# An exponential split between ScalarE and VectorE: six-pass VectorE blocks, six a unit instead of five, and a shorter accumulator read-out and quantisation

## The reference

```python
xn = _layernorm(x)
q, k, v = (split_heads(xn @ w.T + b) for w, b in ...)      # 16 heads of 16; q is divided by sqrt(16)
attn = softmax(einsum('bhqd,bhkd->bhqk', q, k))            # 4096 x 4096 for each head
ctx = einsum('bhqk,bhkd->bhqd', attn, v)
x_fp8 = clip(xn * scale, -448, 448).astype(float8_e4m3fn)  # the same for the weight
out = x + (ctx @ out_w.T + out_b) + ((x_fp8 @ w_fp8.T) * scales + bias)
```

## Time and profile before

| | us |
|---|---|
| median of 3 runs | 1886.2 (1885.57 to 1886.49) |
| span of the profiled execution, first to last instruction | 1883.1 |
| outside the span, against the median | 3.1 |
| ScalarE's exponentials, first start to last end | 108.9 to 1840.2 |
| busy: PE, DVE, ACT | 1648.8, 1552.4, 1764.1 |

### The profile page before, as it was taken

How to read it: one execution, slowest core, us unless ns; L and a number is a source line. 1 busy time by engine, 2 the same in 40 slices (tenths; PEclk the granted TensorE clock), 3 DMA queues, 4 the chain that set the end, 5 groups by cost and what they waited for, 6 DMA issues and landing times.

```text
span 1883.1 us, 74604 instructions
## 1 busy us (share of the span) xinstructions
PE 1648.8 (88%) x33418; PEld 558.0 (30%) x33418; DVE 1552.4 (82%) x1908; ACT 1764.1 (94%) x1944; POOL 41.1 (2%) x57
## 2 busy tenths in 40 slices
PE   7988888888888888888888888888888888888888
PEld 4632222222222222222222222222222222222226
DVE  8687878878787888878787987878888887878786
ACT  2389999999999999999999999999999999999990
POOL 0000000000000000000000000000000000000003
PEclk9999999999999999999999999999999999999999
DMA  7420100000000100000010000001000000001003
GB/s 202 154 90 10 32 10 22 13 18 24 18 24 10 24 13 16 24 18 24 10 31 8 17 20 18 24 10 31 10 22 12 18 24 18 24 10 26 13 14 107
DMA packets 94966, 57.20 MB, mean 30 GB/s; under 512 B 55280, under 2 KB 87280, under 8 KB 94640
## 3 DMA queue, kind: packets, MB, share of 16 engines
q1 hardware_dynamic: 94160, 52.18, 10.3%
q10 hardware_dynamic: 480, 0.20, 0.0%
HBM read 30.54 MB, written 17.30 MB: 25 GB/s over the span
## 4 chain that ended last, share of the span: by engine, by line
ACT 48%; issue 37%; PE 11%; DVE 1%; POOL 1%; ACTq 1%; DMA 0%; SPq 0%; POOLq 0%; DVEq 0%
ACT probs L679 48%; PE banks L1308 3%; PE banks L1164 3%; PE banks L1267 3%; PE banks L1175 1%; ACTq L678 1%; DVE o_junk L963 1%; DVE o_sb L962 1%; POOL o_sb L600 0%; PE banks L1148 0%; POOL o_junk L600 0%; DMA qk_bias<-in_L_attn_k_b_dram 0%; DVE bits L983 0%; DVE w_max L764 0%; DVE xn_all L833 0%
## 5 line engine op out<-in xcount | busy, mean ns | idle before, releaser
L679 ACT ACTIVATE probs<-banks 128x1024 f32<-128x1024 f32 x1888 | 1731.0, 1193 | 0.3 <-PE banks L1267 0.2
L1308 PE MATMUL banks<-probs,v_st 64*32 64x512 f32 x15104 | 1004.5, 590 | 2.2
L1267 PE MATMUL banks<-q_st,k_st 50*32 50x512 f16 x16384 | 793.3, 381 | 211.9 <-ACT probs L679 208.9
L1267 PEld LDWEIGHTS banks<-q_st,k_st 50*32 50x32 f16 x16384 | 233.5, 89 | 1145.3 <-ACT probs L679 1088.8
L996 DVE SCALAR_TENSOR_TENSOR horner<-horner,bits 128x1024 f32<-128x1024 f32 x320 | 393.1, 1228 | 11.0
L1308 PEld LDWEIGHTS banks<-probs,v_st 64*32 64x32 f32 x15104 | 272.3, 106 | 66.4 <-DVE o_junk L963 11.4
L983 DVE TENSOR_SCALAR bits<-banks 128x1024 int32<-128x1024 f32 x160 | 195.9, 1225 | 76.9 <-PE banks L1267 76.8
L996 DVE SCALAR_TENSOR_TENSOR horner<-bits 128x1024 f32<-128x1024 f32 x160 | 196.1, 1226 | 5.5
L1001 DVE SCALAR_TENSOR_TENSOR d_probs<-horner,powers 128x1024 f32<-128x1024 f32 x160 | 196.0, 1225 | 5.5
L962 DVE COPY o_sb<-banks 128x512 f32<-128x512 f32 x32 | 22.1, 692 | 130.9 <-PE banks L1308 98.0
L992 DVE TENSOR_SCALAR bits<-bits 128x1024 int32<-128x1024 int32 x160 | 111.1, 694 | 5.5
(11 more groups left out here) (103 smaller groups left out, 435.6 us busy)
## 6 DMA issues: line engine op xcount, KB each, us to landing
k_st<-k_parts SPq DMA_DIRECT2D x102, 64.0 KB, 2.2
q_st<-q_parts SPq DMA_DIRECT2D x198, 32.0 KB, 1.9
k_st<-k_parts SPq DMA_DIRECT2D x102, 60.0 KB, 2.2
q_st<-neg_row SPq DMA_DIRECT2D x264, 1.0 KB, 1.7
xnT_copy<-probs SPq DMA_DIRECT2D x8, 512.0 KB, 3.1
q_parts<-x8T SPq DMA_DIRECT2D x16, 256.0 KB, 2.9
k_parts<-x8T SPq DMA_DIRECT2D x16, 256.0 KB, 2.4
w_f<-xnT_copy SPq DMA_DIRECT2D x16, 256.0 KB, 2.9
```

The lines of the kernel that those rows point to most:

```text
L679: act.activation(probs[:, at:at + WIDE * CHUNK].rearrange("p (t c) -> p t c", t=WIDE), banks[:, bank:bank + WIDE, :], ACT.Exp, bias=EXP_SHIFT,
L1267: last = pe.matmul(banks[cols, bank + g, :], k_st[rows, keys], blocks[rows, j], start=True, stop=True, tile_position=(g * GROUP, t * VCOLS))
L1308: last = pe.matmul(banks[VCOLS * qb:VCOLS * (qb + 1), 6 + half, cols], v_st[keys, kt, :], src[keys, g * CHUNK:(g + 1) * CHUNK][:, cols], s ...
```

## The change

Four things, all in VectorE's program and in the constants:

1. `d_block` has six passes instead of seven: out of the bank into integers (as before), one mask (fraction bits), then four two-operand passes, three on f32 for a cubic in the fraction and a last one that adds it, scaled, to the integer words and writes int32 into `d_probs` read as int32. The first pass now waits for the last pass of the block before it, since that reads the same words. ScalarE's bias (`EXP_SHIFT`) changes to fit.
2. `D_AT` gets a sixth place and closer spacing, `(10, 22, 30, 38, 46, 54)`, and `D_PAIRS` a sixth pair: 58 exponentials a unit on ScalarE, 6 blocks on VectorE. `order`, `sums_at` and the counts follow from these tables.
3. `take_sums` transposes bank 6 and then bank 7 out of PSUM (the second frees the accumulators) and adds them afterwards in SBUF, only 17 of every 32 columns.
4. `quantise` folds its subtraction and its clamp into one pass: five passes instead of six.

```diff
-    D_AT = (9, 23, 33, 43, 53)
+    D_AT = (10, 22, 30, 38, 46, 54)
-    D_PAIRS = ((KT // 2 - 1, 0), (KT // 2 - 1, 1), (KT - 1, 0), (KT - 1, 1), (KT - 2, 0))
-    D_STEPS = 5
+    D_PAIRS = ((KT // 2 - 1, 0), (KT // 2 - 1, 1), (KT - 1, 0), (KT - 1, 1), (KT - 2, 0), (KT - 2, 1))
+    D_STEPS = 4
...
-                step(dve.tensor_scalar(y, src, s, None, ALU.mult))
+                step(dve.tensor_scalar(y, src, s, -FP8_MAX, ALU.mult, ALU.max))
...
-                step(dve.tensor_tensor(y, r, c, ALU.subtract))
-                return dve.tensor_scalar(dst, y, FP8_MAX, -FP8_MAX, ALU.min, ALU.max)
+                return dve.scalar_tensor_tensor(out=dst, in0=r, scalar=LARGEST_ROUNDED, in1=c, op0=ALU.min,
+                                                op1=ALU.subtract)
...
-                    chain(dve.tensor_copy(o_sb[:, :], banks[:, 6, :]), link0 + 1)
-                    dve.scalar_tensor_tensor(out=o_junk[:, :], in0=banks[:, 7, :], scalar=1.0, in1=o_sb[:, :],
-                                             op0=ALU.mult, op1=ALU.add, accum_out=o_inf[:, span(h * 2 + u, 1)]
-                                             ).then_inc(c.acc_free, 1)
+                    chain(dve.transpose(o_sb[:, :], banks[:, 6, :]), link0 + 1)
+                    dve.transpose(o_junk[:, :], banks[:, 7, :]).then_inc(c.acc_free, 1)
                     dve.wait_ge(c.acc_free, h * 2 + (u + 1 + ACC_0))
-                    chain(dve.transpose(o_sb[:, :], o_junk[:, :]), link0 + 2)
+                    used, other = (t.rearrange("p (t v) -> p t v", v=VCOLS)[:, :, 0:DH + 1] for t in (o_sb, o_junk))
+                    chain(dve.scalar_tensor_tensor(out=used, in0=other, scalar=1.0, in1=used, op0=ALU.mult,
+                                                   op1=ALU.add, accum_out=o_inf[:, span(h * 2 + u, 1)]), link0 + 2)
...
+                    to = slice(n % 2 * HALF, (n % 2 + 1) * HALF)
                     if n:
-                        dve.wait_ge(c.d_chain, steps)
+                        dve.wait_ge(c.d_ready, done)
                     dve.wait_ge(c.st_done, h * c.head_places + (at + 1))
...
-                    dve.tensor_scalar(tops[:, :], words[:, :], EXPONENT_BITS, None, ALU.bitwise_and
+                    dve.tensor_scalar(fraction[:, :], words[:, :], MANTISSA_BITS, None, ALU.bitwise_and
                                       ).then_inc(c.d_chain, 1)
                     dve.wait_ge(c.d_chain, steps + 1)
-                    dve.tensor_scalar(words[:, :], words[:, :], MANTISSA_BITS, ONE_BITS, ALU.bitwise_and,
-                                      ALU.bitwise_or).then_inc(c.d_chain, 1)
-                    for j in range(3):
-                        dve.wait_ge(c.d_chain, steps + (2 + j))
-                        dve.scalar_tensor_tensor(out=horner[:, :], in0=(horner if j else bits)[:, :], scalar=POLY[j],
-                                                 in1=bits[:, :], op0=ALU.add, op1=ALU.mult).then_inc(c.d_chain, 1)
+                    dve.scalar_tensor_tensor(out=horner[:, :], in0=fraction[:, :], scalar=CURVE_ROOT,
+                                             in1=fraction[:, :], op0=ALU.add, op1=ALU.mult).then_inc(c.d_chain, 1)
+                    dve.wait_ge(c.d_chain, steps + 2)
+                    dve.scalar_tensor_tensor(out=powers[:, :], in0=fraction[:, :], scalar=CURVE_SLOPE,
+                                             in1=horner[:, :], op0=ALU.mult, op1=ALU.add).then_inc(c.d_chain, 1)
+                    dve.wait_ge(c.d_chain, steps + 3)
+                    dve.scalar_tensor_tensor(out=horner[:, :], in0=powers[:, :], scalar=CURVE_BASE,
+                                             in1=horner[:, :], op0=ALU.add, op1=ALU.mult).then_inc(c.d_chain, 1)
...
-                    dve.scalar_tensor_tensor(out=d_probs[:, n % 2 * HALF:(n % 2 + 1) * HALF], in0=horner[:, :],
-                                             scalar=POLY[3], in1=powers[:, :], op0=ALU.add, op1=ALU.mult
-                                             ).then_inc(c.d_ready, 1)
+                    dve.scalar_tensor_tensor(out=d_probs.bitcast(I32)[:, to], in0=horner[:, :], scalar=CURVE_SCALE,
+                                             in1=words[:, :], op0=ALU.mult, op1=ALU.add).then_inc(c.d_ready, 1)
```

More of the change, by code:

```diff
@@ L35 @@
 ROUND_TO_3_BITS = 1.5 * 2.0 ** 20
+LARGEST_ROUNDED = FP8_MAX + 256.0 * ROUND_TO_3_BITS
 EXPONENT_BITS = 0x7F800000
+FRACTION = 2.0 ** 23
 PARTS = 2
@@ L51 @@
 LOG2E = 1.4426950408889634
-ONE_BITS = 0x3F800000
 MANTISSA_BITS = 0x007FFFFF
-EXP_BIAS = 1013270912.0
-EXP_SHIFT = -EXP_BIAS / 2.0 ** 23 / LOG2E
-POLY = (-0.1511656492948532, 12.309608459472656, 23.089841842651367, 37.712982177734375)
+EXP_BIAS = 127.0
+EXP_SHIFT = -EXP_BIAS / LOG2E
+CURVE_ROOT = -1.00001524 * FRACTION
+CURVE_SLOPE = 5.89161538 * FRACTION
+CURVE_BASE = 22.8639511 * FRACTION ** 2
+CURVE_SCALE = 0.0134250815 * FRACTION ** -3
 WIDE = 2
@@ L97, in program @@
     SCALE = float(DH) ** -0.5
-    UNIT = LOG2E * 2.0 ** 23
+    UNIT = LOG2E * FRACTION
     NORM = float(D) ** 0.5
@@ L896, in quantise_weight @@
                 dve.wait_ge(xq_used, 1)
-            QUANT_STEPS = 6
+            QUANT_STEPS = 5
             qn = [0]
@@ L978, in d_block @@
                     bank = take_bank(h, at)
-                    words, tops = bits.bitcast(I32), powers.bitcast(I32)
+                    words, fraction = bits.bitcast(I32), powers.bitcast(I32)
+                    to = slice(n % 2 * HALF, (n % 2 + 1) * HALF)
                     if n:
-                        dve.wait_ge(c.d_chain, steps)
+                        dve.wait_ge(c.d_ready, done)
                     dve.wait_ge(c.st_done, h * c.head_places + (at + 1))
@@ L986, in d_block @@
                     dve.wait_ge(c.d_taken, taken_at(h, u, D_AT[n]))
-                    if n:
-                        dve.wait_ge(c.d_ready, done)
-                    dve.tensor_scalar(tops[:, :], words[:, :], EXPONENT_BITS, None, ALU.bitwise_and
+                    dve.tensor_scalar(fraction[:, :], words[:, :], MANTISSA_BITS, None, ALU.bitwise_and
                                       ).then_inc(c.d_chain, 1)
                     dve.wait_ge(c.d_chain, steps + 1)
-                    dve.tensor_scalar(words[:, :], words[:, :], MANTISSA_BITS, ONE_BITS, ALU.bitwise_and,
-                                      ALU.bitwise_or).then_inc(c.d_chain, 1)
-                    for j in range(3):
-                        dve.wait_ge(c.d_chain, steps + (2 + j))
-                        dve.scalar_tensor_tensor(out=horner[:, :], in0=(horner if j else bits)[:, :], scalar=POLY[j],
-                                                 in1=bits[:, :], op0=ALU.add, op1=ALU.mult).then_inc(c.d_chain, 1)
+                    dve.scalar_tensor_tensor(out=horner[:, :], in0=fraction[:, :], scalar=CURVE_ROOT,
[6 more added lines that the diff above has]
+                                             in1=horner[:, :], op0=ALU.add, op1=ALU.mult).then_inc(c.d_chain, 1)
                     dve.wait_ge(c.d_chain, steps + D_STEPS)
```

## The result

The changed kernel takes 1923.1 us (1922.7 to 1924.3) beside 1886.35 us for the kernel before: a ratio of 1.0199, 95% interval 1.0185 to 1.0214. It is 36.8 us slower; the forecast said 45 us slower (1931 us, range 1918 to 1943), by the same path.

What follows compares the result with a forecast made beforehand. ScalarE's exponentials bound the kernel; late VectorE blocks would stall them, 1.4 us a unit over 32 units. 1883.1 + 45.2 - 0.2 - 0.2 = 1928 of span, with 3.1 outside 1931 us; range 1918 to 1943, chance 0.8.

Steps and rivals of the forecast that it cites:

- What bounds the kernel: Attention part: ScalarE's unbroken exponentials, 0.917 us each, set the clock; VectorE's 0.5 us idle ahead of blocks is the slack.
- A block's period, 7.03 us: VectorE's six-pass block: 6.83 us of passes plus six gaps of 0.035, when blocks follow without idle time.
- the rival of dearer passes: VectorE's new block passes: +0.06 on the last gives 1939 us; int32 halving its rate gives 2068, chance 0.04.
- the fast one: VectorE blocks: seven exponentials cover a block (period at most 6.42 us), no lateness accumulates, 1867 us; chance 0.09.
- a period of 6.67: VectorE's block period from which the faster rival decides: four steps there cost as much as the exponential saves.
- The 4 x 0.36 = 1.4: The sum given as what four block steps cost at the faster rival's deciding block period.
- The unit, 55.5 us: Maxima to maxima: 2.35, four periods 28.12, first pass and release 1.29, then 23.80; 1.4 us more than 54.09.
- the 0.06 taken off: Unit sum of 55.56 taken as 55.5, for half the shortening (up to 0.17) of an exponential finding the pipeline drained.
- The allowance, about 1 us, and the stalls: First passes about 1 us late delay nobody; ScalarE stalls 0.6 at 41, 49, 57, 0.5 around 23 and 33.
- Part 3: Accumulator read-out by two transposes: 1.47 us instead of 1.42 until free, addition 0.44, -0.2 us in the whole kernel.
- Part 4: Quantisation's subtraction and clamp become one pass of 0.69 to 0.75, -0.4 us, hidden; at most 0.4 once.
- The rest of VectorE's unit: VectorE's other work still fits: 1.5 us idle ahead of the read-out, more than 0.7 ahead of the next block.

Runs made afterwards that it cites:

- e1: Changed kernel with the five old places (9, 23, 33, 43, 53), keeping six-pass blocks, new read-out and new quantisation: 1885.8 us, ratio 1.000.
- e3: Changed kernel with one of a block's four two-operand passes left out (the one adding the curve's base), same places: 1864.3 us, ratio 0.9885.
- e5: e4 with the bias addition that ended the quantisation piece moved behind the accumulators' read-out: 1859.1 us, ratio 0.9856 to the kernel before.
- e8: Changed kernel with two buffers for the integer words, so a first pass need not wait for the preceding block's last pass: 1907.7 us, ratio 1.0117.
- e2: Kernel before with only the six new places (10, 22, 30, 38, 46, 54), blocks keeping seven passes: 2004.0 us, ratio 1.063.
- e4: Changed kernel with its six blocks at places 9, 23, 32, 40, 49, 58: 1891.8 us, ratio 1.003.
- e6: Changed kernel without its block at place 54, five blocks at 10, 22, 30, 38, 46: 1934.6 us, ratio 1.026.

## Why the prediction was right, and where its sizes were off

- **What bounds the kernel**: right. ScalarE at 0.917 us an exponential, and a late first pass of VectorE as what holds it up: e1 and e3 have blocks that wait for their scores, and the loss is not there. But idle time ahead of a block is more than is needed. e5 has next to none (37.0 us ahead of all its 192 first passes, nearly all of it at places 9 and 23), and no exponential waits; what counts is that no block is later than the allowance.
- **A block's period, 7.03 us**: measured 874.27 - 867.25 = 7.02. The pass that no row showed, int32 beside f32 with int32 out, takes 1.225 us, like its neighbours; so does the one that reads the fraction as int32. With that the rival of dearer passes is out, and so is the fast one, which needed a period of 6.67. (The 4 x 0.36 = 1.4 beside it is what four steps give back between 7.03 and 6.67, not what they cost at 6.67.) The rival's support, the Trainium skill's 75 ns of fixed cost an instruction (Vector Engine (DVE) Microarchitecture Reference, "Measured stream behaviour on trn2"), is for instructions that queue without waits; in e8 two neighbours without a wait start 908.20 - 907.06 = 1.14 apart, where chained ones stand 1.26 apart, so for the unchained pair the trace agrees with it.
- **The unit, 55.5 us**: measured 55.25. The terms, as forecast and as measured: maxima to the block at 22, 2.35 and 2.23; four periods, 28.12 and 28.06; first pass, release and the stretch to the next maxima, 25.09 less the 0.06 taken off, and 24.97. All three were high, by 0.12, 0.06 and 0.06. The first is a step I missed: the block's first pass doesn't wait for the last of the maxima's instructions, so it starts at 846.21 while that runs until 846.29; I had added a gap where there is an overlap. The same kind of overlap is what e2 showed and e8 bought, and the trace of before had it too. There the last step of `quantise` (L728), which the next one doesn't wait for, runs until 866.63, and the addition behind it (L1048) starts at 866.54:

```profile
866.20 0.43 DVE L728 TENSOR_SCALAR x8T<-horner 128x512 bf16<-128x512 f32 x1
```

  In the third I took 0.06 off for the exponential that finds the pipeline empty, and the stretch is 0.12 shorter; that this exponential is the whole reason isn't shown. Together it is 0.25 us a unit, 8 us of the kernel: 45 forecast, 37 measured.
- **The allowance, about 1 us, and the stalls**: 2.3 forecast, 2.07 measured (55.25 - 53.18). Stalls of 0.60 at 41, 49 and 57 came as said. At 33 there is none: the block at 30 starts 1.2 us late and nobody waits, so the allowance is 1.2, not 1, and the forecast that blocks are past it from place 30 on was wrong by one step. The 0.25 at place 23 is there, and e3 isolates it.
- **Part 3**: accumulators freed in 0.72 + 0.72 with a gap, the addition on 272 columns at 0.44, and nothing of it seen in the time. Right, e1.
- **Part 4**: the new last pass takes 0.69; hidden. Right for this kernel. That its cover was 1.5 us was in the text (1.39 measured), and that the first sum would wait without it. That such a wait can be followed by a lower clock was not; e4 shows what losing the cover costs.
- **The rest of VectorE's unit**: idle 1.67 us ahead of the block at place 10, where the text had more than 0.7, and 0.91 ahead of the maxima, as before.

## What to carry to other kernels

When work is handed from one engine to another at fixed places in a rotation, compare the period of the receiving engine with the time that the giving engine needs between two places, step by step: here 7.02 against 6.42 us, four times in a row, turned a possible gain of 29 us into a loss of 37 (8 us of the difference lie at place 23), although the receiving engine was idle 5.7 of 55 us a unit. The mean load doesn't tell: six blocks fit in one placing with VectorE 88% busy (e5), and five at 74% don't in another (e6). And an instruction that nobody waits for may still stand ahead of one that somebody does: moving a 0.69 us addition behind the accumulators' read-out was worth 33 us.

## What the runs showed of the hardware that was not expected

- A standstill of TensorE of 1.8 us in an otherwise dense stream was followed, in twelve of fifteen cases, by some 3 us at a granted clock of 0.50, the 1.2 GHz level; that cost 1.5 us each time, more than the 1.0 of the wait itself (e4). The changed kernel's waits of 0.53 us and e2's of up to 1.2 us had no such drop: from 120 to 1840 us both kernels show a granted clock of 1.00. What decides between the twelve and the three stays open.
- An addition of two tensors on VectorE took 0.90 us instead of 0.69 when a GpSimd copy of 0.40 us ran at the same time, in fifteen of fifteen cases; the sixteenth addition, with no copy beside it, took 0.69 (e4). A placing can bring two such instructions together that never met before.
- Two VectorE instructions of 1.2 us with no wait between them overlap by 0.08 us; with a semaphore wait there is a gap of 0.035. Where the chain sets the time, this 0.12 us a block is worth 15 us (e8).
- A break in ScalarE's stream of exponentials costs 0.10 us on top of the idle time that the profile shows: seven exponentials between two breaks fill 6.52 us, and in the unbroken stream 7 x 0.917 = 6.42.
